# A fused attention and linear kernel on one core: in the second step, one projection goes ahead of the scores, and VectorE takes part of a copy

## What is computed

```python
Q = (layernorm(x) @ Wq.T + bq)      # and K, V from ctx, each (b, s, 16 heads, 32)
score = einsum('bshd,bsgd->bshg', Q, K)           # 16 x 16 for each token
attn = einsum('bshg,bsgd->bshd', softmax(score), V).reshape(b, s, 512)
x = x + tanh(g_xattn) * (attn @ Wo.T + bo)
x = x + tanh(g_ffn) * (layernorm(x) @ (Wf * scale[:, None]).T + bias)
```

## Time and profile before

| | before |
|---|---|
| median of 3 runs | 281.3 us (280.01 to 281.74) |
| profiled execution, its own time | 281.8 us |
| its span, first to last instruction | 280.1 us |
| TensorE busy | 267.5 us (96%) |
| VectorE, ScalarE, GpSimd busy | 198.8 (71%), 144.5 (52%), 88.4 us (32%) |
| mean granted TensorE clock | 0.994 of 2.4 GHz |

### The profile page before, as it was taken

One profiled execution on the slowest core, in us unless ns is written; L12 is line 12 of the kernel. 1 busy time (PEld: TensorE's weight loads), 2 busy tenths in 40 slices (PEclk: granted clock), 3 DMA queues, 4 the chain that ended last, 5 costly groups with the idle time before them and its releaser, 6 DMA issues.

```text
span 280.1 us, 8653 instructions
## 1 busy us (share of the span) xinstructions
PE 267.5 (96%) x3516; PEld 235.9 (84%) x3516; DVE 198.8 (71%) x331; ACT 144.5 (52%) x276; POOL 88.4 (32%) x80
## 2 busy tenths in 40 slices
PE   7899998498999999999999999999999999999995
PEld 7789997397978898888988899889988998887775
DVE  2775569189885987569774987579773855598884
ACT  4755543853686236643387225933289432954700
POOL 4104000032157116422183024612183031802722
PEclk9999999899999999999999999999999999999999
DMA  6997769991887764894488853986478729263203
GB/s 204 351 382 226 208 247 249 258 232 56 274 248 237 147 225 150 235 220 139 160 232 247 191 195 130 240 225 156 181 201 246 158 77 231 74 128 72 104 37 112
DMA packets 71912, 53.83 MB, mean 192 GB/s; under 512 B 36688, under 2 KB 59984, under 8 KB 71888
## 3 DMA queue, kind: packets, MB, share of 16 engines
q1 hardware_dynamic: 71744, 52.97, 65.6%
q10 hardware_dynamic: 144, 0.52, 0.5%
HBM read 34.08 MB, written 19.40 MB: 191 GB/s over the span
## 4 chain that ended last, share of the span: by engine, by line
PE 69%; DMA 10%; SPq 7%; ACT 7%; DVE 3%; issue 3%; DVEq 0%; ACTq 0%
PE acc L496 55%; PE score_ps L496 4%; PE score_ps L616 3%; DMA raw_spare<-wq_t 3%; ACT late L796 3%; PE attn_ps L638 3%; PE turn_ps L530 2%; DMA v_scratch<-v_or_norm 2%; SPq L350 2%; DMA k_rows<-k_scratch 2%; DMA q_pad<-q_scratch 2%; SPq L398 1%; SPq L335 1%; DVE turned L1002 1%; DMA q_scratch<-q_t 1%
## 5 line engine op out<-in xcount | busy, mean ns | idle before, releaser
L796 ACT ACTIVATE late<-attn_ps 32x256 f32<-32x256 f32 x124 | 46.6, 376 | 6.1 <-PE attn_ps L638 3.2
L496 PE MATMUL acc<-ctx_parts,wk_parts 128*128 128x256 f32 x384 | 48.7, 285 | 0.3 <-DVE late L1079 0.2
L496 PEld LDWEIGHTS acc<-ctx_parts,wk_parts 128*128 128x128 f32 x384 | 47.1, 191 | 1.7 <-issue 0.8
L1242 POOL TENSOR_TENSOR rstd<-var_eps,minus_half 128x1 f32<-128x1 f32 (+1 forms) x24 | 17.5, 728 | 95.3 <-DVE var_eps L937 95.3
L496 PE MATMUL acc<-wv_parts,ctx_parts 128*128 128x512 f32 x192 | 46.0, 394 | 0.8 <-ACT wv_parts L720 0.8
L496 PEld LDWEIGHTS acc<-wv_parts,ctx_parts 128*128 128x128 f32 x192 | 35.4, 188 | 8.1 <-issue 1.0
L496 PE MATMUL acc<-xa_parts,wq_parts 128*128 128x256 f32 x336 | 41.1, 281 | 0.1
L496 PE MATMUL acc<-wo_parts,xa_parts 128*128 128x512 f32 x168 | 40.4, 395 | 0.6 <-ACT xa_parts L720 0.6
L496 PEld LDWEIGHTS acc<-xa_parts,wq_parts 128*128 128x128 f32 x336 | 40.2, 188 | 0.7 <-DVE xa_parts L913 0.5
L496 PEld LDWEIGHTS acc<-wo_parts,xa_parts 128*128 128x128 f32 x168 | 31.0, 188 | 7.9 <-ACT xa_parts L720 1.0
L496 PE MATMUL acc<-wf_parts,x_parts 128*128 128x512 f32 (+1 forms) x132 | 29.7, 380 | 0.1
(11 more groups left out here) (89 smaller groups left out, 377.7 us busy)
## 6 DMA issues: line engine op xcount, KB each, us to landing
ctx_raw<-ctx_t SPq DMA_DIRECT2D x8, 512.0 KB, 4.7
x_norm<-x SPq DMA_DIRECT2D x8, 512.0 KB, 5.2
k_scratch<-k_t SPq DMA_DIRECT2D x8, 512.0 KB, 3.7
k_rows<-k_scratch SPq DMA_DIRECT2D x32, 128.0 KB, 3.4
q_pad<-q_scratch SPq DMA_DIRECT2D x32, 128.0 KB, 3.2
v_scratch<-v_or_norm SPq DMA_DIRECT2D x32, 128.0 KB, 2.2
v_keys<-v_scratch SPq DMA_DIRECT2D x16, 256.0 KB, 4.3
x_res<-x SPq DMA_DIRECT2D x8, 512.0 KB, 3.8
```

What stands on the lines that cost most here:

```text
L496: last = pe.matmul(dst, left(a, k), right(b, k), start=(n == 0), stop=(n == len(terms) - 1))
L796: nc.scalar.activation(attn_rows(t, q), attn_block(t, q), ACT.Identity).then_inc(a_out, 1)
L1242: nc.gpsimd.tensor_tensor(rstd[which][:, t], var_eps[which][:, t], minus_half[:, t], ALU.pow).then_inc(n_rstd[which], count)
```

## The change

TensorE computes K(2) before score(1) where it did so after it. VectorE copies the second tile of the attention of chunk 0 (8 pieces), which ScalarE did. VectorE makes the low part of that chunk's first tile and scales the rows `bo_row` and `bf_row` at the end of its step 0, and no longer in the middle of step 1. ScalarE copies the first tile before it lays the keys of chunk 1. VectorE makes the low part of ctx(2) between `v_bias(1, 0)` and `v_bias(1, 1)`, and `turned_lo(xa_parts, ..., 2)` ahead of `softmax_b(1)`. `x1_apply(3)` goes behind both tiles of `turned_lo(x2_parts, ..., 0)`. F(0) waits for the low part of Wf only where it uses it: it takes low-part weights last.

Work, sizes and transfers stay the same. The counts that other engines wait for follow the new owner of the copies (`act_moves`).

The new count, the new owner of the copies, and TensorE's order:

```diff
+        def act_moves(c):
+
+            return 0 if first(c) else MOVES * c - MOVES // TILES
...
+            if first(c):
+                owner = "act" if tile == 0 else "dve"
+                return range(tile * each, (tile + 1) * each) if engine == owner else ()
...
             def tensor_step(i):
                 if final(i - 1):
                     return last_tensor_step(i)
+                if first(i - 1):
+                    k_layer(2, "v", 1)
                 score(i)
...
                 elif first(i - 1):
-                    k_layer(2, "v", 1)
                     pe.wait_ge(w_lo, pieces_to(WO, 1))
                     o_layer(0, "k", 2)
                     q_layer(2, "o", 0)
...
                 if exists(i - 1) and not late_f(i - 1):
-                    if not exists(i - 2):
-                        pe.wait_ge(w_lo, pieces_to(WF, 1))
                     f_layer(i - 1, "v", i + 1)
```

The waits of F(0) on Wf, inside `f_layer`:

```diff
+                    if first(c) and t == 0:
+                        pe.wait_ge(w_hi, pieces_to(WF, 1))
...
+                           w_low_ready=(lambda: pe.wait_ge(w_lo, pieces_to(WF, 1))) if first(c) else None)
```

ScalarE, steps 0 and 1:

```diff
                     ctx_high(2)
-                    lay_keys(1)
                     act.wait_ge(gates_in, 2 * DMA)
                     nc.scalar.activation(tanh_g[:], gates[:], ACT.Tanh).then_inc(gates_done, 1)
-                    x1_high(2)
                     attn_copy(0, 0)
                     attn_high(0, 0)
-                    k_bias(2, (0,))
+                    lay_keys(1)
+                    x1_high(2)
+                    k_bias(2)
+                    attn_high(0, 1)
                     return
-                if first(i - 1):
-                    attn_copy(0, 1)
-                    attn_high(0, 1)
-                    k_bias(2, (1,))
-                else:
+                if not first(i - 1):
```

VectorE, the end of step 0 and step 1:

```diff
                 v_bias(1, 0)
+                ctx_low(2)
                 v_bias(1, 1)
-                ctx_low(2)
-
-            def second_step():
-                scores_turn(1)
-                softmax_a(1)
+                attn_some(0, 1)
                 attn_low(0, 0)
                 dve.wait_ge(consts_in, 2 * DMA)
                 dve.wait_ge(gates_done, 1)
                 for row, n in ((bo_row, 0), (bf_row, 1)):
                     nc.vector.tensor_scalar(row[:], row[:], tanh_g[:, n:n + 1], None, ALU.mult).then_inc(rows_scaled, 1)
+
+            def second_step():
+                scores_turn(1)
+                softmax_a(1)
+                attn_low(0, 1)
+                turned_lo(xa_parts, x1_hi, x1_lo, 2)
                 softmax_b(1)
-                turned_lo(xa_parts, x1_hi, x1_lo, 2)
-                attn_low(0, 1)
                 spread_first(1)
...
                 w_low(WF, 0)
+                turned_lo(x2_parts, x2_hi, x2_lo, 0, (0,))
+                w_low(WF, 1)
+                turned_lo(x2_parts, x2_hi, x2_lo, 0, (1,))
                 x1_apply(3)
-                w_low(WF, 1)
-                turned_lo(x2_parts, x2_hi, x2_lo, 0)
                 v_bias(2, 0)
```

More of the change, by code:

```diff
@@ L804, in attn_high @@
                 if final(c):
-                    act.wait_ge(a_out, MOVES * c + QH * (GROUPS // TILES + tile))
+                    act.wait_ge(a_out, act_moves(c) + QH * (GROUPS // TILES + tile))
                     if tile == 1:
-                        act.wait_ge(a_out_dve, QH)
+                        act.wait_ge(a_out_dve, MOVES // TILES + QH)
+                elif first(c) and tile == 1:
+                    act.wait_ge(a_out_dve, MOVES // TILES)
                 else:
-                    act.wait_ge(a_out, MOVES * c + MOVES // TILES * (tile + 1))
+                    act.wait_ge(a_out, act_moves(c) + MOVES // TILES * (tile + 1))
                 high(at_parts(c)[:, HI, :, P * tile:P * (tile + 1)],
```

6 lines of the change are left out of this document (4 added, 2 removed).

## The result

| | before | after |
|---|---|---|
| median of four runs each | 280.83 us (280.01 to 281.74) | 284.52 us (283.11 to 285.83) |
| ratio after to before | | 1.0113, 95% interval 1.0071 to 1.0156 |
| profiled execution: its time, its span | 281.8, 280.1 us | 285.83, 284.1 us |
| mean granted TensorE clock in it | 0.994 | 0.982 |

The 281.3 from which the forecast starts is the median of three runs of before; with the fourth, 280.36, it is 280.83. The change makes the kernel 3.7 us slower, where 1.0 was forecast. Two of the four runs of after took 283.11 and 283.29 at a mean clock of 0.994 and 0.993, the other two 285.75 and 285.83 at 0.981 and 0.982. The profiled one is among the slower pair, and no run took the 284.5 of the median, which is the mean of the two in the middle. Comparisons leave out a few launches with a disturbance of their own.

A forecast was written before the change was run, and what follows sets the result against it. TensorE, busy 96% of the span, was taken as the bound, so only the start of F(0) counted: 0.95 us later, added to the 281.3 us median, gave 282.3 us, with a range of 280.3 to 284.6.

The forecast's parts named there:

- slower by over 1%: Whole kernel: a measured time above 284.1 us, given a chance of 0.16.
- the three signs: Prediction wrong if Q(2) follows o(0) without a gap, VectorE doesn't wait for x2_high(0), or the clock falls in F(0).
- VectorE's wait for `x2_high(0)`: VectorE ahead of F(0): it waits about 2 us, from about 75.9 to 78.1, for ScalarE's x2_high(0).
- the gate: Ahead of F(0): VectorE's chain, ending in v_bias(2, 0), decides when F(0) may start.
- the sum of the work: Up to F(0): the chain through o_residual, x2_high(0) and v_bias(2, 0) starts F(0) at 83.2, 0.95 us later than before.
- The step that failed: Q(2) behind its gap: runs 1.2 us slower, V(2) ends at 80.9, nothing below changes because ScalarE is busy until 74.3.
- the gap of 3.7 us: TensorE between o(0) and Q(2): it waits from 62.2 to 65.9 for VectorE's o_residual.
- rival B: Ahead of F(0): the clock falls in a gap of 3.5 or 2.3 us, costing 1.2, 283.5 us; chance 0.17.
- What was forecast in pieces: Single times: score(1) from 54.95, o_residual from 65.15, VectorE's wait from about 75.9 to 78.1, VectorE's copies costing nothing.
- The price of `x1_apply(3)`: VectorE ahead of F(0): 1.96 us net, first tile undisturbed, second at 1.47 beside GpSimd; bounds 0.92 and 2.85.
- Rival A: VectorE ahead of F(0): x1_apply(3) is undisturbed by GpSimd, F(0) starts at 82.1, 281.2 us; chance 0.15.
- rival C: Ahead of F(0): GpSimd goes first, x1_apply(3) takes 2.9 us and the clock falls, 284.4 us; chance 0.12.

The follow-up runs named there:

- e7: The changed kernel with K(2) put back behind score(1) on TensorE, the rest kept: 289.5 us against 282.17, ratio 1.025.
- e10: The changed kernel with GpSimd's x2_bias(0) made to wait until x1_apply(3) is done: 282.57 us against 281.4, ratio 1.0037.
- e11: The changed kernel with SyncE's loads of scale_row and Wf issued behind the load of V(1): 284.19 us, ratio 1.0109.
- e5: The changed kernel with 10 instead of 12 small warm-up matmuls at the start: 284.61 us against 282.17, ratio 1.0082.
- e1: The changed kernel again, unaltered: four runs of 289.09, 286.02, 282.29 and 286.23 us against 281.84, ratio 1.0111.
- e8: The changed kernel, unaltered, run once more for a second profile: 284.77 us.
- e3: The changed kernel with 2 wide warm-up matmuls instead of 12 small ones at the start: 287.82 us against 281.84.
- e2: The changed kernel with x1_apply(3) back ahead of both tiles of turned_lo(x2_parts, 0): 281.86 us against 281.84, ratio 1.0003.
- e6: The changed kernel with K(2) in halves around score(1), o_residual(0, 0) ahead of spread_first(1), x1_apply(3) put back: 283.4 us against 282.17, ratio 1.0037.
- e12: The changed kernel with the second split of K(2) and scale_row and Wf loaded behind V(1): 279.87 us against 280.95, ratio 0.995.
- e4: The kernel before with one edit, K(2) ahead of score(1) on TensorE: 281.76 us against 281.84, ratio 1.0025.
- e9: The changed kernel with K(2) split around score(1), ScalarE's and VectorE's queues matched to it, x1_apply(3) put back: 280.49 us against 281.4, ratio 0.9958.

## Why the prediction was right, and where it was not

**How near the number came, and how much of that is luck.** 284.52 lies 0.08 us inside the upper end of the range (284.6), and the lower of the two kinds of run, near 283.2, and the higher, near 285.8, were drawn twice each. Three of one kind would have put the median at one of them, and 285.8 is outside. The ratio of 1.0113 falls in "slower by over 1%", which had 0.16. And two of the three signs that the prediction gave for being wrong came: Q(2) follows o(0) without a gap, and in the first profile the clock falls in F(0). Of the three, only VectorE's wait for `x2_high(0)` was as foretold.

**The direction, the gate and the sum of the work were right.** The following table shows it. It has the time from the start of chunk 2's turns to the start of F(0), from the timelines of the kernel before and of the six profiles that have TensorE's new order, `x1_apply(3)` where the change puts it and GpSimd free to start beside it (e7 lacks the first, e10 the last):

| profile | gap of TensorE | what ran behind it | turns to F(0) |
|---|---|---|---|
| before | 4.16 ahead of score(1) | as the earlier trace rows | 34.06 |
| forecast | 3.7 ahead of Q(2) | | 35.03 |
| e11 | 3.67 ahead of Q(2) | Q(2) in 5.94 | 34.74 |
| e5 | 3.64 in o(0) | 14 of o(0) in 3.47 | 34.80 |
| e1 | 3.30 in o(0) | 18 of o(0) in 5.95 | 35.29 |
| e8 | 4.65 in o(0) | 18 of o(0) in 5.76 | 36.41 |
| after | 3.46 in o(0) | 18 of o(0) in 7.18 | 36.74 |
| e3 | 3.69 ahead of Q(2) | Q(2) in 8.76 | 36.90 |

Where the clock stayed up, the sum holds within 0.3 us, with the stop (e5) as without it (e11). Where it fell, F(0) is later than forecast, by 0.3 (e1, a short stop and about half of the loss in the 18 matmuls) to 1.9 us, wherever the gap stands. In e8 the length of the stop counts too: it is 4.65, and o(0) holds up both residuals.

**The step that failed** is this one, on the gap of 3.7 us: "I take it that Q(2) runs 1.2 us slower; that makes V(2) end at 80.9 and changes nothing below, since ScalarE is busy until 74.3 anyway". The 1.2 was taken from the stall of the earlier trace rows. Behind a gap of this size the profiles that fell lose between 1.4 and 3.0 (5.76 and 7.18 for 4.33, 8.76 for 5.80). In after and e3 the low level lasts longer: the earlier trace rows has it for 3.4 us, after for all of 62 to 68. In e8 it lasts no longer (0.73 on average over 5.6 us is about 3 us of it), and still the 18 wide matmuls lose 1.43, where half of the 3.4 us in the earlier trace rows fell on score(1), whose small matmuls lost 0.36. And it is on the path. In after the slow matmuls are o(0)'s, and `o_residual(0, 1)` reads them. In e3 they are Q(2)'s, and ScalarE, which was to be "busy until 74.3 anyway", waits 1.38 us for them until 76.85. The term that the sum lacked is 0.3 to 1.9, 1.7 in the profiled run of after.

**The second term that was too small is the clock in F(0).** That is rival B, with 0.17 and a price of 1.2. It is 1.48 in the first profile, behind a gap of 2.57, and absent in e2 and e10, where the gap is 0.72 and 1.47. It isn't there in every run of after either (e1 and e8 have gaps of 2.46 and 2.58 and full clock), nor behind the 3.31 of e5 and the 3.22 of e11. The time follows the clock in the main: in the first result and the repeat, runs at a mean clock of 0.993 or 0.994 took 282.3 to 283.3, and those at 0.980 to 0.982 took 285.8 to 286.2, with the 289.09 apart. The exceptions are 286.02 at 0.988 and, with the longest stop, 284.77 at 0.994 (e8). The forecast of 282.3 is the time of a good run: one of the nine runs of this kernel is below 283, and five are above 285.

**What was forecast in pieces was met.** With the 0.45 of the later start taken off: score(1) 54.95 (54.90), `o_residual(0, 0)` 65.15 (64.98), VectorE's wait for `x2_high(0)` 2.2 (2.41). The copies on VectorE cost nothing: 3.62 us, and VectorE waits another 2.05 behind them for score(1).

**The price of `x1_apply(3)` was right in size and mechanism:** 1.96 forecast, 1.95 measured, 1.00 with GpSimd held back (e10) and in its old place (e2). Rival A, 1.00, and rival C, 2.9, are out: GpSimd started 0.16 behind VectorE (82.87 against 82.71) and got its turn between the two tiles. In the trace the first tile takes 0.54, as alone, and the second 1.49, which are the two terms of the forecast. The Trainium skill's page "SBUF — State Buffer", section "Who interferes with whom", has the port pair held for a whole instruction. The case agrees with each of the two tiles as an instruction of its own.

**The gap was in another place than forecast, by a mechanism that I had not seen: TensorE ran out of instructions.** I asked of each matmul whether its operands were there, and never whether the instruction was. e3 and e5 show that the place of the stop follows the count of instructions ahead of it (20 and 4 matmuls further on for 20 and 4 fewer), and e11 that the stop goes when the transfers beside it are moved. The traces show the same from the other side. In each of the ten profiles with a stop (after, e1 with two, e2 to e6, e8 to e10) TensorE goes on 1.4 to 1.7 us after an instruction packet has landed. With the loads of Wf beside it, the packet for the place in o(0) starts 3.9 to 6.7 us behind the start of score(1); with the transfer engines idle it starts 0.4 (e11, 55.27) and 1.4 us (e12, 54.59) behind it, and has landed before o(0) reaches the place. So it is the packet that comes late. The order gives the reason that it came with the swap (e4): score(1) is 128 small matmuls with a weight load each, 256 instructions in 1.6 us, and in the kernel before, K(2), 96 instructions in 6.7 us, stood between it and the seam in o(0), the border between two blocks. The DMA view of the kernel before, from 57.9 to 59.2, has an instruction packet too (`q8 instruction: 1, 0.02, 4.2%`), under transfers as dense, and TensorE didn't stop: it reached the sixth matmul of o(0) only at about 63.3. The distance from the seam in score(0) to the one in o(0) is 14 + 24 + 24 + 128 + 8 + 48 + 128 + 6 = 380 matmuls, with a load each 760 instructions. The Trainium skill's page "Advanced Engine Details and Errata", section "ISA Cache", gives lines of 16 KB or 256 instructions; three of them are 768. The case agrees: the packet is 0.02 MB, and in e1 three packets move from the end of the first stop to the end of the second. The 8 that are missing may be waits, which I didn't count. Why only every third border stops TensorE, no run shows.

**What stays open.** Why the clock falls behind some gaps and not behind others as long. Why the packet moves when it does, and came no sooner with large matmuls ahead of it (e5, e9): the trace doesn't show when it is asked for. Whether the stop adds anything to after's median: it takes the place of a gap ahead of Q(2) that would be as long, and the ratios with and without it (1.0111, 1.0109) are the same. In single profiles it does hold up `o_residual(0, 0)`, by 0.65 (e8), 0.24 (e10) and 1.42 us (e9).

## What to carry to other kernels

Price a new gap on TensorE by the slow stretch behind it as well, in two sizes, and follow who reads the slow matmuls: here both lie on the path, and with the clock in F(0) they made 1.0 us into 3.7. If a gate behind a wait decides the end, put the work that nobody waits for into the wait and not behind it: that one line (e2) was worth all that the change had lost. And when a burst of small matmuls is moved, look at what stands right behind it: here a stop marked `issue`, at a place that shifted when instructions were taken out far ahead of it, was TensorE waiting for its next block of instructions, which came through the same transfer engines as the data.
